# The graph kernel's node-by-edge selections: the node numbers as a second tensor operand in place of a scalar one

## The reference, cut to what matters

```
layer 1 (8 heads) and layer 3 (2 heads):          # attention over the edges
    alpha = (q[dst] * k[src]).sum(per head)
    ex    = exp(alpha - segment_max(alpha, dst)[dst])
    agg   = segment_sum(v[src] * ex / denom[dst], dst)
layer 2 (twice, 8 edge types):                    # a mean over each (dst, type)
    msg   = h[type, src]
    mean  = segment_sum(msg, dst * 8 + type) / max(count, 1)
    agg   = mean.sum(over types)
```

## Time and profile before

| | |
|---|---|
| runs | median 6029.29 us of 3 (6024.53 to 6030.99) |
| span of the profiled execution | 7205.4 us; the page gives no other time of that execution |
| PE busy | 4349.8 us (60%) |
| DVE busy | 3857.3 us (54%) |
| ACT busy | 1461.9 us (20%) |
| POOL busy | 4079.2 us (57%) |
| the three groups of `selt` on DVE, 52 operations each | 39.2, 43.3 and 39.3 us |

### The profile page before, as it was taken

How to read it: one execution, slowest core, us unless ns; L and a number is a source line. 1 busy time by engine, 2 the same in 40 slices (tenths; PEclk the granted TensorE clock), 3 DMA queues, 4 the chain that set the end, 5 groups by cost and what they waited for, 6 DMA issues and landing times. The chain is left out here.

```text
span 7205.4 us, 86034 instructions
## 1 busy us (share of the span) xinstructions
PE 4349.8 (60%) x19030; PEld 3531.2 (49%) x19030; DVE 3857.3 (54%) x11927; ACT 1461.9 (20%) x3928; POOL 4079.2 (57%) x4191
## 2 busy tenths in 40 slices
PE   4777778746566656795666666344343456665656
PEld 4666666635555555444444444233333345555555
DVE  7444444446566656745555555344444455666655
ACT  4122222212222222350111111000000112222222
POOL 1666666646566554106666665666666555555553
PEclk9977776766666666897888888555555566667676
DMA  2433333323333334274444444122222333333333
GB/s 49 126 108 102 100 101 100 100 87 109 106 108 107 105 99 84 82 286 125 135 129 136 128 136 109 51 60 56 59 56 59 74 100 113 106 110 113 108 112 64
DMA packets 426775, 738.44 MB, mean 102 GB/s; under 512 B 100523, under 2 KB 280580, under 8 KB 419701
## 3 DMA queue, kind: packets, MB, share of 16 engines
q0 software_dynamic: 173200, 436.47, 23.0%
q1 hardware_dynamic: 244484, 289.62, 12.2%
q10 hardware_dynamic: 8592, 6.82, 0.3%
HBM read 613.55 MB, written 120.20 MB: 102 GB/s over the span
## 5 line engine op out<-in xcount | busy, mean ns | idle before, releaser
L1637 POOL DMA_INDIRECT xh<-pair_d,src_i x1658 | 1647.5, 994 | 1191.6 <-issue 459.2
L2648 POOL DMA_INDIRECT l2e_rows<-msg_d,msg_i x829 | 804.8, 971 | 749.3 <-POOLq L61 315.4
L999 POOL DMA_INDIRECT l0e_rows<-node_d,src_i x829 | 789.0, 952 | 450.4 <-issue 220.4
L854 POOL DMA_INDIRECT l2f_rows<-msg_d,msg_i x829 | 782.7, 944 | 431.4 <-issue 231.9
L1156 PE MATMUL l0e_ps<-l0e_rows,l0e_sel 128*128 128x256 f32 x1664 | 795.2, 575 | 282.3 <-issue 232.8
L888 PE MATMUL l2f_ps<-l2f_rows,l2f_sel 128*128 128x128 f32 x1664 | 413.1, 417 | 600.1 <-DVE xh L919 501.0
L2766 PE MATMUL l2e_ps<-l2e_rows,l2e_sel 128*128 128x256 f32 x1664 | 490.0, 427 | 422.5 <-DVE l2e_sel L2860 396.4
L888 PEld LDWEIGHTS l2f_ps<-l2f_rows,l2f_sel 128*128 128x128 f32 x1664 | 367.3, 310 | 674.7 <-issue 394.9
L2825 DVE TENSOR_TENSOR l_acc<-l_acc,l2e_ps 128x256 f32 x832 | 349.4, 420 | 498.4 <-DMA node_d<-l1t_queries 329.0
L919 DVE TENSOR_TENSOR xh<-xh,l2f_ps 128x128 f32 x832 | 238.3, 286 | 675.5 <-DMA tb_raw<-edges_d,starti 470.7
L1221 DVE TENSOR_TENSOR early_acc<-early_acc,l0e_ps 128x264 f32 x832 | 356.8, 429 | 441.0 <-PE l0e_ps L1157 168.6
(11 more groups left out here) (454 smaller groups left out, 8180.8 us busy)
## 6 DMA issues: line engine op xcount, KB each, us to landing
l0e_rows<-in_edge_attr_dram SPq DMA_DIRECT2D x832, 64.0 KB
msg_d<-l1t_queries SPq DMA_DIRECT2D x50, 1024.0 KB, 3.9
l1te_local<-local_d SPq DMA_DIRECT2D x52, 512.0 KB
l2e_local<-local_d SPq DMA_DIRECT2D x52, 512.0 KB
l3te_local<-local_d SPq DMA_DIRECT2D x52, 512.0 KB
xh<-pair_d,src_i POOLq DMA_INDIRECT x1658
msg_d<-l2e_msg SPq DMA_DIRECT2D x50, 512.0 KB
l0e_rows<-node_d,src_i POOLq DMA_INDIRECT x829
```

The costliest lines, as they stand in the source:

```text
L854: pool.indirect_dma_start(rows[:, t % R, :], None, table, bass.IndirectOffsetOnAxis(index[:, t:t + 1], 0)) \
L999: pool.indirect_dma_start(rows[:, t % R, 0:D], None, table, bass.IndirectOffsetOnAxis(g.src_i[:, t:t + 1], 0)).then_inc(gathered[t % R], 16)
L1637: pool.indirect_dma_start(rows[:, t % R, :], None, g.pair_d, bass.IndirectOffsetOnAxis(g.src_i[:, t:t + 1], 0)).then_inc(gathered[n % RG], 16)
L2648: pool.indirect_dma_start(rows[:, t % R, :], None, table, bass.IndirectOffsetOnAxis(index[:, t:t + 1], 0)).then_inc(gathered[t % R], 16)
```

## The change

The comparison that writes `selt` is issued as an operation of two tensors. The scalar operand, one 32-bit value per partition, becomes a second tensor operand: the same column, repeated 2048 times with a step of zero. The first operand, the output, the waits and the semaphore stay. The edit stands in two places, in `attention_edges` (both walks) and in `gather_relations`.

```diff
@@ -1876,8 +1876,8 @@
                     dve.wait_ge(local_in[s % 2], 16 * (s // 2 + 1))
                     if s >= 2:
                         dve.wait_ge(widened, s - 1)
-                    nc.vector.tensor_scalar(selt[:, s % 2, :, :].rearrange("p s e -> p (s e)"), local[:, s % 2, :],
-                                            g.tile_f[:, 0:1], None, ALU.is_equal).then_inc(selt_made, 1)
+                    nc.vector.tensor_tensor(selt[:, s % 2, :, :].rearrange("p s e -> p (s e)"), local[:, s % 2, :],
+                                            g.tile_f[:, 0:1].broadcast_to([P, S * P]), ALU.is_equal).then_inc(selt_made, 1)
```

## The result

The changed kernel takes 6237.35 us (median of 5 runs, 6231.11 to 6243.90). The kernel before took 6030.99 us beside it (6024.53 to 6031.57). The ratio is 1.0346, with a 95% interval of 1.0335 to 1.0358: 206 us slower. Forecast were 6214 us, 185 more.

A forecast was written before the change was run, and what follows sets the result against it. It took POOL's gathers and the DVE-PE ring to be close together as bounds in the runs. Walks 135 us plus layer 2's pass 50 us gave 185 us on the 6029 us median: 6214 us, range 6115 to 6285 us.

The forecast's parts named there:

- The price: Selection comparison on DVE: 2.30 us per operation, from 0.754 in walks and 0.832 in layer 2; 237 us of VectorE time.
- The inference that the runs go at POOL's pitch: In the runs POOL waits far less than in the profile; a round of 16 tiles lasts near 20.0 us.
- What the walks pay: Both walks: the later of ring (1.55 us a round) and held gathers (1.0); taken as 1.3, 135 us.
- the ring: DVE and PE waiting for each other in the walks: almost all 1.55 us appear each round, 161 us at most.
- the gathers' term: POOL's gathers beside selections lose 1.0 us more a round in walks, 1.4 in layer 2: 180 us in all.
- The 1.3: Walks: us taken per round, between 1.0 (POOL) and 1.55 (ring); 104 rounds give 135 us.
- Layer 2's pass: Layer 2's first pass: longer DVE partly covered by POOL's pace, gathers' loss stays; 0 to 76 us, 50 taken.
- The signs: Selections 2.2 to 2.4 us; PE's carry load waiting for DVE in most walk rounds; gathers beside selections 2 to 3 us.
- Rival 3: Faster: POOL sets the pace, DVE's extra time is idle time, new form releases held gathers; 54 us less, 5975 us; chance 0.04.
- Rivals 1, 2 and 4: Respectively: ring and held gathers add, 6286 us, chance 0.12; comparison takes 1224 ns, 6085 us, 0.06; all covered, 6029 us, 0.05.
- rival 4: Extra DVE time covered and gathers lose what they lost before: 6029 us, no change; chance 0.05.

The follow-up runs named there:

- second profile: The kernel before, profiled again with no edit, to set against the profile of the changed kernel: 6028.74 us, ratio 0.9999; the profiled execution spans 6027.1 us.
- with one tensor: Kernel before with its scalar comparison also keeping a running sum, in walks and layer 2, so one SBUF tensor is read: 6040.70 us, ratio 1.0019.

## Why the prediction was right in its number, and where its steps were not

- **The price** was right: 2.30 us forecast, 2.288 measured; the three stretches gain 80.0, 82.9 and 77.2 us of DVE time, 80 forecast, and DVE as a whole 239.6, 237 forecast.
- **The inference that the runs go at POOL's pitch** was right. The second profile of the kernel before has 1063.4 / 52 = 20.4 us a round in the walk and 20.2 in layer 2's pass, 20.0 forecast.
- **What the walks pay** was the step that failed, though its sum came out near (135 us forecast, 138 measured). "Almost all 1.55 us appear" of the ring was wrong: 1.65 us more of DVE in every round cost 11 us with one tensor. I had taken the ring of the earlier trace rows for a bound of the runs, against my own inference from the pitch; with POOL at its pitch in both stages, the gathers' term alone should have stood. The 1.3 was a mean of two terms, one that the change does not pay at all and one that was too small; that it came within 3 us is luck.
- **The gathers' term** was mis-sized. It was forecast at 1.0 us a round in the walks and 1.4 in layer 2, 180 us together; the groups give 139.2 / 104 = 1.34 and 65.9 / 52 = 1.27, 205 us. The scaling (0.65 us for each microsecond of comparing) was the wrong law. The right one was in the rows: in the earlier trace rows the gather ends at 1985.92 and the selection at 1985.11; in the earlier trace rows the ends are 3806.38 and 3805.58, then 3810.50 and 3809.68. All three stand 0.80 to 0.82 us apart. With that law 2.30 us give 1.55 less the old form's 0.17 in every round, some 215 us.
- **Layer 2's pass** was forecast at 50 us, two thirds of a term "between 0 and 76"; 61 measured. There too the cover was no cover: what POOL loses, nobody gives back.
- **The signs.** PE's carry load does wait in most rounds (50 of 52, 101.1 us), as forecast, and the sign was worthless: with one tensor it waits 114.7 us at almost no loss. The gathers of 2 to 3 us were seen, and they were the sign that mattered.
- **Rival 3** needed two things. Its first came true: DVE's round has over 1.55 us that hardly anybody waits behind. Its second did not, since the two-tensor form holds the gathers longer than the old one. It rested on my reading of the Trainium skill, page "SBUF — State Buffer", section "SBUF: two separate sides": an operation with two SBUF inputs shuts out only a GpSimd operation that reads SBUF. I took a gather for one that mostly doesn't. The traces agree with the rule if a gather counts as one that reads, but only at its start: one that begins under the two-tensor form stands until that is over, and one that is under way goes on (46 of 46). They agree too in what the other forms hold: the old form, which reads one tensor at 0.77 us for 2048 elements, holds gathers of both kinds, and the one-tensor form at 2.34 us, three times slower, holds none. The Trainium skill's page gives the shared ports to an operation in a two-port mode and to one with two SBUF inputs; the old form would be the first, the change the second, and the slow form neither. No run shows the ports or the modes themselves. That it is the second SBUF input, and not something else in a two-tensor instruction, no kernel was made to try; but the products and the weighing, whose second operand lies in PSUM, hold no gather in the trace of the change (301 cases).
- **Rivals 1, 2 and 4** fall: the two prices did not add (the change costs 206 us, all of it in the gathers), the price was not 1224 ns, and nothing covered the hold. The 257.1 us of unexplained waits that spoke for rival 4 are not among the waits of the second profile.

## What to carry to other kernels

Ask first which engine's list runs without a break in an ordinary execution; a microsecond taken from that one is paid in full, and a microsecond on the others only beyond their slack. Where it is POOL with its gathers, choose a VectorE form by what it holds and not by how long it takes: here 2.34 us with one tensor cost 11 us in the whole program, and 1.22 us with two cost 45. And when one operation stands under another in a few rows, compare the ends, not only the lengths: a constant distance between the ends, here 0.82 us, says that one waits for the other to be over, and such a wait does not grow with the share of time.

## What the runs showed that I had not expected

- A running sum beside the scalar comparison takes it from 0.77 to 2.34 us, and adds 0.08 us to read the sum; in return no gather is held.
- The hold goes both ways, but not alike. Where a gather begins within 0.03 us of the selection's start, ahead of it or behind, it goes free and the selection of two tensors waits: it takes up to 2.355 us in place of 2.285, and its end stands 1.38 us after the gather's end each time (nine cases in the change). So a gather keeps this form out for some hundredths of a microsecond of its 0.95, while the form keeps a later gather out until it is over. The old form waits for a later part of a gather too: the 26 old selections that begin 0.47 to 0.68 us into one end 0.51 to 0.52 us after it, and take 0.78 to 0.99 us in place of 0.75. The Trainium skill's page cited above lets whoever starts first hold the ports for the whole instruction; these traces show that for VectorE's side alone.
- Two halves issued one behind the other let the waiting gather in between (115 of 130), though their records overlap by 0.07 to 0.09 us.
